# A gated recurrence with block attention on one core: bias rows from one small transfer, spread by TensorE

## What is computed

```python
gi = x @ W_ih + b_ih
gh = h @ W_hh + b_hh
r = sigmoid(i_r + h_r);  z = sigmoid(i_z + h_z)
n = tanh(i_n + r * h_n)
h = (1 - z) * n + z * h                      # 64 steps, one after the other
x = x + hs                                   # all states h
block_repr = x summed over blocks of 8 steps
keys = rmsnorm(block_repr @ Wk.T) * rms_weight;  scores = keys . cond[1]
proj = (softmax(scores) @ block_repr) @ Wo.T
out = x + layernorm(x + proj) * gamma + beta
```

## Time and profile before

| | us |
|---|---|
| three runs | 375.1, 376.13, 377.11 |
| the profiled execution, whole | 375.67 |
| its span in the profile | 373.5 |
| PE busy | 359.5 (96%) |
| DVE busy | 264.4 (71%) |
| ACT busy | 158.6 (42%) |
| POOL busy | 15.6 (4%) |

### The profile page before, as it was taken

How to read it: one execution, slowest core, us unless ns; L and a number is a source line. 1 busy time by engine, 2 the same in 40 slices (tenths; PEclk the granted TensorE clock), 3 DMA queues, 4 the chain that set the end, 5 groups by cost and what they waited for, 6 DMA issues and landing times.

```text
span 373.5 us, 9797 instructions
## 1 busy us (share of the span) xinstructions
PE 359.5 (96%) x3269; PEld 211.1 (57%) x3269; DVE 264.4 (71%) x1138; ACT 158.6 (42%) x506; POOL 15.6 (4%) x47
## 2 busy tenths in 40 slices
PE   8988999999999999999999999999999999997994
PEld 5545655566665556666555666655566665434662
DVE  2927667677676778686768767676778676778896
ACT  4402326262534344352526262534344364766510
POOL 5013000000000000000000000000000000100000
PEclk9999999999999999999999999999999999999999
DMA  8985544423232322324141323232232322110038
GB/s 278 409 321 147 170 103 148 110 60 100 72 98 70 96 67 55 98 58 110 43 105 41 98 70 98 70 98 70 68 79 70 98 55 70 47 43 18 22 144 307
DMA packets 28100, 40.05 MB, mean 107 GB/s; under 512 B 3120, under 2 KB 19120, under 8 KB 28080
## 3 DMA queue, kind: packets, MB, share of 16 engines
q1 hardware_dynamic: 28080, 39.79, 36.7%
HBM read 19.60 MB, written 4.19 MB: 64 GB/s over the span
## 4 chain that ended last, share of the span: by engine, by line
PE 85%; DVE 6%; DMA 5%; SPq 1%; issue 1%; ACT 1%; DVEq 0%
PE gates_ps L601 43%; PE gi_ps L570 36%; DMA gcx<-in_w_ih_dram 2%; DMA w_hh<-in_w_hh_dram 2%; DVE gcx L1082 1%; PE third_ps L601 1%; PE keys_ps L601 1%; PE fourth_ps L601 1%; DMA h_tok<-hist 1%; DVE w_hh L998 1%; PE gi_ps L583 1%; PE keys_ps L711 1%; SPq L268 0%; DVE zh L874 0%; DVE turned L804 0%
## 5 line engine op out<-in xcount | busy, mean ns | idle before, releaser
L601 PE MATMUL gates_ps<-w_hh,turned 128*32 128x384 f32 x1920 | 167.3, 489 | 0.6 <-DVE turned L804 0.5
L601 PEld LDWEIGHTS gates_ps<-w_hh,turned 128*32 128x32 f32 x1920 | 56.5, 109 | 85.6 <-issue 56.4
L570 PE MATMUL gi_ps<-w_ih_hi,xt_hi 128*128 128x384 f32 x240 | 86.7, 363 | 0.0
L570 PE MATMUL gi_ps<-w_ih_hi,xt_lo 128*128 128x384 f32 x240 | 80.7, 338 | 0.0
L570 PE MATMUL gi_ps<-w_ih_lo,xt_hi 128*128 128x384 f32 x240 | 79.7, 334 | 0.0
L460 ACT ACTIVATE rz<-gates_ps 128x256 f32<-128x256 f32 x60 | 23.1, 385 | 128.9 <-PE gates_ps L601 128.7
L868 DVE TENSOR_TENSOR rz<-gates_ps,rz 128x128 f32<-128x128 f32 x60 | 17.5, 291 | 79.5 <-ACT rz L460 79.5
L570 PEld LDWEIGHTS gi_ps<-w_ih_hi,xt_hi 128*128 128x128 f32 x240 | 44.9, 187 | 37.5 <-issue 36.9
L570 PEld LDWEIGHTS gi_ps<-w_ih_lo,xt_hi 128*128 128x128 f32 x240 | 45.1, 188 | 0.0
L570 PEld LDWEIGHTS gi_ps<-w_ih_hi,xt_lo 128*128 128x128 f32 x240 | 44.9, 187 | 0.0
L804 DVE STREAM_TRANSPOSE turned<-hist 128x32 f32<-128x32 f32 (+1 forms) x192 | 36.8, 217 | 2.2
(11 more groups left out here) (209 smaller groups left out, 292.3 us busy)
## 6 DMA issues: line engine op xcount, KB each, us to landing
gi<-gi_tok SPq DMA_DIRECT2D x60, 192.0 KB, 3.4
x1t<-in_x_t_dram SPq DMA_DIRECT2D x16, 256.0 KB, 3.2
gcx<-in_x_tok_dram SPq DMA_DIRECT2D x16, 256.0 KB, 3.2
h_tok<-hist SPq DMA_DIRECT2D x64, 64.0 KB, 2.2
out_dram<-gcx SPq DMA_DIRECT2D x16, 256.0 KB, 2.1
gcx<-in_w_ih_dram SPq DMA_DIRECT2D x4, 768.0 KB, 6.9
w_hh<-in_w_hh_dram SPq DMA_DIRECT2D x4, 768.0 KB, 9.7
wo_t<-in_wo_t_dram SPq DMA_DIRECT2D x1, 1024.0 KB, 5.4
```

What stands on the lines that cost most here:

```text
L570: mm = pe.matmul(gi_ps[tok][:, 0:G3], a[:, k, :], w[:, k, gi_cols(j)], start=(m == 0), stop=(m == 3 * NJ - 1))
L601: mm = pe.matmul(gates_bank(t)[j * B:(j + 1) * B, P:], before[:, k * B:(k + 1) * B], chunk(w_hh, k, j), start=False, stop=(k == NJ - 1), s ...
```

## The change

- The bias rows come as one transfer of 8 rows x 512 floats (16 KB), issued by ACT as its first instruction. Rows 0 to 3 hold, for each j, `b_ih` in the order n, r, z and zeros; rows 4 to 7 hold zeros, and the r, z and n parts of `b_hh`.
- POOL makes first of all a mask `own_rows` (8 x 128: a one where row modulo 4 equals j), and PE multiplies it with the 8 rows (contraction over 8): the sum of both biases appears in all partitions of the recurrence layout. DVE copies it to `bias_rec`. This product takes the place of four of the seven multiplications with zeros.
- DVE adds `bias_rec` to the four banks after k = 0, not after k = 1; all four `split_w` come after that.
- After k = 1 PE makes the input bias `b_in`: four products with 32 rows of contraction (`same_b` by `bias_rec`, one for each j, each in its own row tile of the array and its own PSUM bank). ACT copies the four results to `b_in`, one ahead of its last chunk of `w_ih_hi`, three behind it.
- SP's four bias transfers of 96 KB and the two of 768 KB and 512 KB are gone, POOL's four sums too.
- The two wq products are made by DVE in step 2 of the recurrence, no longer by POOL.

Core of the diff:

```diff
@@ SP
             load_w_ih(1)
-            for j in range(NJ):
-                sp.dma_start(bias_in_rec[j * B:(j + 1) * B, :], bias_d[j:j + 1, :].broadcast_to([B, 6 * P])
-                             ).then_inc(bias_in, 16)
             load_w_ih(2)
...
-            sp.dma_start(b_in[:], b_ih_d.rearrange("j n -> (j n)")[None, :].broadcast_to([P, 3 * D])
-                         ).then_inc(b_in_loaded, 16)
-            sp.dma_start(b_hh_rz.rearrange("p j n -> p (j n)"), b_hh_rz_d[None, :].broadcast_to([P, 2 * D])
-                         ).then_inc(b_in_loaded, 16)
@@ POOL
+            pool.memset(own_rows, 0.0).then_inc(own_made, 1)
+            own = own_rows.rearrange("p (j b) -> p j b", j=NJ)
+            for half_ in range(2):
+                pool.wait_ge(own_made, 1 + half_)
+                pool.affine_select(out=own, in_=own, compare_op=ALU.not_equal, fill=1.0, base=-NJ * half_,
+                                   pattern=[[-1, NJ], [0, B]], channel_multiplier=1).then_inc(own_made, 1)
...
-                pool.tensor_tensor(rz_cols, rz_cols, b_hh_rz[:, j, :], ALU.add).then_inc(b_in_ready, 1)
-            pool.wait_ge(b_in_ready, NJ)
-            pool.wait_ge(consts_in, 16 * (NJ + 2))
-            pool.tensor_tensor(wq, wq, rms_tok, ALU.mult).then_inc(wq_ready, 1)
-            pool.tensor_tensor(wq_rec, wq_rec, rms_rec, ALU.mult).then_inc(wq_ready, 1)
@@ ACT
+            def keep_b_in(j):
+                act.activation(b_in[:, gi_cols(j)], b_in_ps[j][:, 0:G3], ACT.Copy).then_inc(b_in_ready, 1)
+            act.dma_start(bias_rows, bias_d).then_inc(bias_in, 16)
...
                     split_x(1)
+                    act.wait_ge(b_in_laid, NJ)
+                    keep_b_in(0)
                 act.wait_ge(w_ih_in[k], 16)
                 act.activation(w_ih_hi[:, k, :], w_stage[:, k, :], ACT.Copy).then_inc(w_hi_ready, 1)
+            for j in range(1, NJ):
+                keep_b_in(j)
@@ PE
-            keep_warm(7).then_inc(pe_warmed, 1)
+            keep_warm(1)
+            pe.wait_ge(own_made, 3)
+            pe.wait_ge(bias_in, 16)
+            pe.matmul(small_ps[:], own_rows, bias_rows, start=True, stop=True).then_inc(bias_laid, 1)
+            keep_warm(2).then_inc(pe_warmed, 1)
...
-                    if k == 2:
+                    if k == 1:
                         pe.wait_ge(first_seeded, t + 1)
...
-                    if k == 1:
+                    if k == 0:
                         mm.then_inc(first_laid, 1)
+                if k == 1:
+                    pe.wait_ge(made, 8 + 3 * NJ)
+                    for j in range(NJ):
+                        rows = slice(j * B, (j + 1) * B)
+                        pe.matmul(b_in_ps[j][:], same_b[rows, :], bias_rec[rows, :], start=True, stop=True,
+                                  tile_position=(j * B, 0)).then_inc(b_in_laid, 1)
@@ DVE
+                if peeled and s == 2:
+                    dve.wait_ge(consts_in, 16 * (NJ + 2))
+                    dve.tensor_tensor(wq, wq, rms_tok, ALU.mult).then_inc(wq_ready, 1)
+                    dve.tensor_tensor(wq_rec, wq_rec, rms_rec, ALU.mult).then_inc(wq_ready, 1)
...
-            split_w(0)
-            dve.wait_ge(bias_in, 16 * NJ)
-            dve.tensor_tensor(bias_rec[:, P:3 * P], bias_rec[:, P:3 * P], bias_in_rec[:, D:], ALU.add
-                              ).then_inc(bias_summed, 1)
-            dve.wait_ge(bias_summed, 1)
+            dve.wait_ge(bias_laid, 1)
+            dve.tensor_copy(bias_rec, small_ps[:]).then_inc(bias_kept, 1)
+            dve.wait_ge(bias_kept, 1)
...
+            split_w(0)
             split_w(1)
```

33 lines of the change are left out of this document (15 added, 18 removed).

## The result

The changed kernel takes 378.72 us (median of seven runs, 376.27 to 379.14), where the kernel before takes 375.49 on the same chip (seven runs, 375.1 to 377.11). The ratio is 1.006, 95% interval 1.0038 to 1.0081: **slower** by 0.6%. (The medians as they stand give 1.0086; the ratio is an estimate from all the runs, and the kernel before has some executions above 376.5.) The forecast was 373.8, range 372.5 to 375.8; it was wrong in direction. The profiled execution of the changed kernel took 376.27 us, span 374.0, and is the fastest of the seven, so its profile shows only a part of the loss. A second profile, further down, shows the rest. One execution of the kernel before, in a later session, took 912.1 us and is left out of all ratios.

A forecast was written before the change was run, and what follows sets the result against it. PE holds 85% of the span, but in the first 37 us transfers bound step 0 and DVE holds up step 2. Gains of 1.24 + 1.09 = 2.33 us take 376.13 to 373.8 us, range 372.5 to 375.8.

The forecast's parts named there:

- The step that failed: At PE's start: the product over 8 rows costs 1.10 us, two with zeros 0.66; x products start at 5.82.
- The bias transfer over ACT: Ahead of PE's first x products: the 16 KB of bias rows land by 3.64 us, so no delay.
- The transfers: At the start, on SP's queue: loads behind the removed bias transfers land 1.76 us earlier; the start gains 1.24 us net.
- The four `b_in` products: On PE behind x chunks 0 and 1: the four run side by side and take 1.07 us for all.
- (c): Rival at the start: the `b_in` products overlap with those of x, transfers are the bound; 373.3 us, chance 0.09.
- (d): Rival at the start: the four `b_in` products run one after the other; 377.0 us, chance 0.04.
- Place 2: Between steps 1 and 2: PE's 1.09 us of idle time, from DVE held by POOL's wq work, goes.
- Rival (b): At the start: ACT's queue waits for SP's loads, x starts 5.85 us late, 379.6 us, low clock adds more; chance 0.07.

The follow-up runs named there:

- after_bias_dma: The changed kernel with SP's four 96 KB bias transfers put back, their data unused; 378.02 us, ratio 1.0049 to the kernel before.
- before_wq_dve: The kernel before with only the two wq products moved from POOL to DVE in step 2; 374.47 us, ratio 0.9975.
- after_fill: The changed kernel with five unread products filling PE's pause behind the last step; 376.94 us, ratio 1.0032 to the kernel before.
- mixed: The kernel before with one small bias transfer on ACT, the 8-row product behind k = 0 and wq on DVE; 374.93 us, ratio 0.9974.
- after_again: The changed kernel with nothing altered, measured again for more executions and a second profile; 378.26 us, ratio 1.004 to the kernel before.

## Why the prediction was wrong, point by point

- **The step that failed** is "The product over 8 rows costs 1.10 us, as the same form with 128 rows does, and two with zeros 0.66", with the start at 5.82 that follows from it and the 2.60 per chunk. 1.10 is a row of the high clock, from the end of the program. 0.33 is a mean over the rise, 2.30 us for seven from 3.42 on the earlier trace rows in an execution that rose at 4.54; the zeros ahead of them start 0.43 apart (2.14, 2.57, 3.00 by PE's timeline), and that is the low pace. Behind both stands a premise of the forecast, that the granted clock is in its top tenth in every slice before, the first included: the first slice averages 9 us and shows nothing of the low clock at its start. At this place the clock is low, and the edit takes away four of the products that raise it. In after's profile: product and zeros 3.15 us for 1.76 (x 1.28 late), first chunk 3.62 for 2.60 (1.02), small change behind it 0.27. Together 2.57 us, by which step 0 ends at 24.89 instead of 22.32. Not all of it is the product's doing: 5.82 was the earliest start of x in any of the profiles, and the seven others with the zeros first have it at 6.27 to 6.61. So by that sample 0.5 to 0.8 of the 1.28 us are lost in most executions without the product too.
- **The bias transfer over ACT**: right. It was there by 3.95, beside 2 MB on SP's queue. By the rule of the page DMA: Bandwidth & Descriptors of the Trainium skill (Queues, rings and completion order) that the prediction cited, the trace agrees.
- **The transfers**: right as landings (chunk 2 of w_ih by 9.46, forecast 9.91; no wait for any chunk, none for w_hh), wrong in worth: about 0.45 us in the profile of after_bias_dma. A PE that ends step 0 at 24.89 would have hidden most of them where they were.
- **The four `b_in` products**: right, 1.07 us (13.40 to 14.47); rivals (c) and (d) fall.
- **Place 2**: right, 5.02 between steps 1 and 2, and faster by itself in before_wq_dve (ratio 0.9975). DVE's wq products fitted the pause. It is nearly all that any of the kernels gained.
- **Rival (b)** had the low clock in it and named a price, but as the result of a late transfer and a pause of PE. The clock was low without any pause. The real rival, "the product that replaces the zeros doesn't lift the clock, and the change takes away the wait that hid it", was missing. It needed only the earlier trace rows read once more: the zeros were there to bring up the clock, and a part that is there for that has a price when it is taken away.
- **What the sum didn't hold at all**: 0.36 us at the loop's end and the clock behind the last step, 1.3 us in the upper group of runs. The range had no room for them. after_fill (376.94 against 378.26) makes it likely that the second is most of the difference between its groups; the remaining 0.3% over before (ratio 1.0032) goes with the start and the loop's end. Why the changed kernel meets the low clock at the end so often is open; the two kernels reach that pause only 0.6 to 1.6 us apart. That the late rise at the start has to do with it is a guess from three profiles.

## What to carry to other kernels

A product that is put where PE is still being brought to its clock is priced at the low clock, and it must be asked whether it does the job of what it replaces: here ten products over 8 rows kept PE busy for 17.4 us, and the clock stayed low. A row of the clock that averages 9 us says nothing of the first 5; the spacing of like products does. When a change removes the wait that is the bound, whatever that wait hid comes due (here a late clock, and POOL's sums that slid into DVE's step), so lay out the next bound with its bad executions, not with the one profile. If a kernel's times fall into two groups, take a profile of each before explaining either.

## What the runs showed of the hardware that was not expected

- Ten float32 products over 8 rows ran 17.4 us without a break at the low clock (0.87 us per record); over 128 rows the clock rose 2.6 us after the first record (at 6.1), and with the other row tiles in use too at 8.3. The Trainium skill, page TensorE: Matmul & The Clock Gate, Part 1, says that the low clock is the default and activity of the array releases it; the runs add that ten products over 8 rows did not.
- Once the clock was high, one product over 8 rows didn't lower it (1.05 us behind k = 0 in mixed, 0.65 per bank after it).
- Behind a pause of 1.65 us PE fell to the low clock for 3.4 us in the profile of after_again (345.3 to 348.7) and not in that of after, the same kernel.
- Kernels that start with the same seven products of zeros had the clock rise anywhere from 4.5 to 7.7 us.
- The trace's record of the granted clock begins at the rise, and the views show 1.00 ahead of it, where like products take twice their later time: 1.29 us for a bank in after, 0.64 behind the rise.
